# Attention scores spread by matmuls into PSUM instead of by two transfers through memory

## The chip, the core and the metric

The kernel runs on one core of a Trainium2 chip. The engines of a core each take their instructions in the order in which the program wrote them, and wait for one another by semaphores: PE multiplies matrices into PSUM, DVE (VectorE) and ACT (ScalarE) work on SBUF and PSUM, POOL (GpSimd) issues gathers and scatters here, SP issues the plain transfers. The metric is the device time of one execution in microseconds (us): the median of the runs.

## What is computed

Four graph layers run one after the other over 10,000 nodes of 512 floats and 2,500 edges (`src`, `dst`), each followed by a layer norm. The change lies in the last one, attention over the edges of a node, in fp32:

```python
q, k, v = jnp.split(x @ W, [Fqk, 2 * Fqk], axis=-1)      # 8 heads of 64
aw = jnp.einsum('ehf,ehf->eh', qs, ks)                   # a score per edge and head
m = jax.ops.segment_max(aw, src, num_segments=n)         # maximum over the edges of a source node
e = jnp.exp(aw - m[src])
denom = jax.ops.segment_sum(e, src, num_segments=n)
alpha = e / denom[src]
out = jax.ops.segment_sum(alpha[:, :, None] * vs, src, num_segments=n)
```

## The kernel before

The edges are cut into T = 20 tiles of 128, one edge per partition. Phases follow one another: `message_phase` (names with m_), `dense_phase` (d_, 80 tiles of nodes), `aggregate_phase`, `edge_rows_phase` (e_), `values_phase` (f_), `attended_rows_phase` (o_). Everything here happens in `values_phase`, a software pipeline written out by hand: STEPS = 24 steps, and in a step each engine works for tiles of different age. With `a = step`, `b = step - 1`, `c = step - 2`, `d = step - 3`, `e = step - 4`:

- Tile a: POOL has gathered the sums of the third layer (L1489, six buffers ahead); PE turns them (`turn_sums`, L1525) and multiplies (`first`, L1544 and L1545); ACT takes logarithms (`logarithms`); DVE finishes the softplus (L1746, L1748).
- Tile b: PE's `second` (L1555, L1558) makes the rows of the third layer, ACT copies them to `y` (L1668), DVE takes the moments (L1754 to L1761), ACT normalises (`x3_rows`).
- Tile c: PE turns the normalised rows (`turn_x3`, L1535) and makes queries into the bank `p_qv`, later keys into the bank `p_k` (L1565 for both and for the values).
- Tile d: DVE multiplies queries and keys and reduces them to 8 scores per edge (`scores`, L1768, L1770). `tile_maximum` then needs, in every partition (edge), the scores of all 128 edges of the tile: it adds `away`, which is very negative for edges of another source node, and takes the maximum (L1779, L1785, L1789). ACT takes the exponential (`weights`, L1694), DVE weighs the values (L1796), PE sums them over equal sources (`tile_sums`, L1594) into `p_S`, two banks.
- Tile e: DVE merges the tile's sums into the running state of a node (`new_maximum` L1804, L1809; `merge` L1817, L1821, L1827). POOL scatters the state to memory (L1500) and, once that has landed, gathers that of the next tile (L1495).

Between these, 40 "pairs" (256 rows of nodes without attention) pass through the same engines: load (L1123, L1124), four wide DVE operations and moments (L1138 to L1161), normalisation on ACT (L1103 to L1171) and store (L1130). `plain_plan` gives steps 0 and 1 three pairs, steps 2 and 3 two, and from step 4 on two and one in turn; DVE does one pair around `weigh_values` and the others at the end of its step, behind `softplus`. p_S holds two banks; p_qv, p_k, p_O, p_R and two p_T take the other six.

The path of the scores from one partition each to all partitions is SP's:

```python
sp.wait_ge(aw_done, t + 1)
sp.dma_start(k.aw_rows[t, :].rearrange("(h p) -> p h", h=HEADS), k.scores[:, t, :]).then_inc(aw_out, 16)
sp.wait_ge(aw_out, 16 * (t + 1))
...
sp.dma_start(spread[:, :, :]..., k.aw_rows[t:t + 1, :].to_broadcast([P, P * HEADS])).then_inc(spread_in, 16)
```

The first transfer writes 1,024 single floats to memory in transposed order; the second reads that row into all 128 partitions. SP's loads and stores of pairs stand behind the two in its queue.

Of the kernel before, what the change touches and what calls it, by code (L numbers as in the profile page):

```python
# [557 lines left out]
def dense_phase(nc, k):  # L558

    k.state = nc.dram_tensor("state", [ROWS, STATE], F32).ap()  # L560
    k.aw_rows = nc.dram_tensor("aw_rows", [EDGE_TILES, P * HEADS], F32).ap()
# [822 lines left out]
def values_phase(nc, k):  # L1384
# [3 lines left out]
    with phase(nc, "f_") as (sb, ps, sem), ExitStack() as ctx:  # L1388
# [11 lines left out]
        spread, prod, q = slots(0, 8).rearrange("p (h e) -> p h e", h=HEADS), slots(8, KB), slots(12, KB)  # L1400
# [4 lines left out]
        away = sb("away", [P, P])  # L1405
# [14 lines left out]
        q_done, q_out, k_done, prod_done, aw_done, aw_out, spread_in, away_done, cand_done, top_done, less_done = (  # L1420
            sem(n) for n in ("q_done", "q_out", "k_done", "prod", "aw", "aw_out", "spread_in", "away", "cand", "top",
                             "less"))
# [23 lines left out]
        def _(sp):  # L1446
# [7 lines left out]
            for step in range(STEPS):  # L1454
                here = HERE[step - 1] if step else 0
                if here > 2:
                    for j in range(pair, pair + here):
                        pair_load(nc, k, sp, j + 2)
                        pair_store(nc, k, sp, j)
                t = step - 3  # L1460
                if 0 <= t < T:
                    sp.wait_ge(aw_done, t + 1)
                    sp.dma_start(k.aw_rows[t, :].rearrange("(h p) -> p h", h=HEADS), k.scores[:, t, :]
                                 ).then_inc(aw_out, 16)
                    sp.wait_ge(aw_out, 16 * (t + 1))
                    if t:
                        sp.wait_ge(cand_done, t)
                    sp.dma_start(spread[:, :, :].rearrange("p h e -> p (h e)"),
                                 k.aw_rows[t:t + 1, :].to_broadcast([P, P * HEADS])).then_inc(spread_in, 16)
                if here <= 2:  # L1470
                    for j in range(pair, pair + here):
                        if j + 2 < PAIRS:
                            pair_load(nc, k, sp, j + 2)
                    for j in range(pair, pair + here):
                        pair_store(nc, k, sp, j)
                pair += here
# [7 lines left out]
        def _(pool):  # L1484
# [20 lines left out]
            gather_state(0)  # L1505
            for step in range(STEPS):
# [11 lines left out]
        def _(pe):  # L1518
# [56 lines left out]
            def keys(t):  # L1575
                pe.wait_ge(turned_out, turn_number(t + 2, 1) + 1)
                if t:
                    pe.wait_ge(prod_done, t)
# [495 lines left out]
```

## Time and profile before

| | us |
|---|---|
| runs, median of 3 | 2539.53 (2536.27 to 2550.1) |
| the profiled execution | 2559.03 |
| its span in the profile | 2557.3 |
| PE busy in the span | 1912.6 |
| DVE busy | 1569.5 |
| ACT busy | 1055.6 |
| POOL busy | 932.2 |

The span is that of one core; 1.7 us of the profiled execution lie outside it. A busy share is a mean over phases which have different limits, so it doesn't tell what bounds one phase. In the trace a tile's name is that of its buffer: `spread`, `prod`, `q` and `srcT` lie in the old buffer `same_dst`, `cand` in `filters`, `dstT` in `column_acc`. PE's rows come in pairs: one fp32 product is two matmul records. "idle before <- releaser" names what ended an engine's idle time.

### The profile page before, as it was taken

What the parts mean: (1) busy time and instruction counts of PE and PEld (TensorE: products, weight loads), DVE (VectorE), ACT (ScalarE), POOL (GpSimd) and SP (SyncE); (2) the same over time, 40 slices, a digit from 0 to 9 for tenths busy, and PEclk for the clock granted to TensorE, in tenths of its full rate; (3) what the DMA queues carried; (4) which work ended last, traced back from release to release, by engine and by line L of the source; (5) the groups of instructions that cost most, each with busy time, mean ns of one, the idle gap of its engine ahead of it and who ended that gap; (6) DMA issues with size and microseconds to landing.
All of it is one profiled execution on the core that took longest, in us unless ns stands there. A gap on an engine that the chain in (4) does not pass through costs nothing. (4 is left out here: it accounts for less than half of the span.)

```text
span 2557.3 us, 23979 instructions
## 1 busy us (share of the span) xinstructions
PE 1912.6 (75%) x5496; PEld 953.9 (37%) x5496; DVE 1569.5 (61%) x2664; ACT 1055.6 (41%) x2019; POOL 932.2 (36%) x1055
## 2 busy tenths in 40 slices
PE   5999995999999999999978603545766666677400
PEld 3444442444444444444434302332333333333200
DVE  5465451777777777777742437976555555555564
ACT  2344342555555555555543212434443333343122
POOL 2211012666665666666646244642011111100023
PEclk9999997999999999999998855556878788888755
DMA  7731024444444444444426342426444444433433
GB/s 250 260 105 38 13 33 117 153 155 145 155 160 149 146 161 157 146 152 161 152 103 199 46 106 69 87 56 245 94 134 114 110 116 116 116 116 108 114 131 111
DMA packets 170013, 326.07 MB, mean 128 GB/s; under 512 B 39889, under 2 KB 53106, under 8 KB 169686
## 3 DMA queue, kind: packets, MB, share of 16 engines
q1 hardware_dynamic: 138438, 244.22, 28.1%
q0 software_dynamic: 28160, 76.53, 13.9%
q10 hardware_dynamic: 3344, 4.51, 0.5%
q8 instruction: 28, 0.46, 0.1%
q14 instruction: 43, 0.35, 0.1%
HBM read 185.35 MB, written 139.84 MB: 127 GB/s over the span
## 5 line engine op out<-in xcount | busy, mean ns | idle before, releaser
L661 PE MATMUL d_p_h<-w3a,d_xT 128*128 128x512 f32 x640 | 290.6, 597 | 25.4 <-DMA d_xT<-in_xT 25.4
L661 PE MATMUL d_p_o<-d_w,d_uT 128*128 128x512 f32 x640 | 289.7, 595 | 3.0 <-ACT d_uT L736 3.0
L661 PE MATMUL d_p_p<-d_wr,d_x1T 128*128 128x512 f32 x640 | 290.6, 597 | 0.0
L818 DVE TENSOR_TENSOR d_zz<-d_yg,d_xbeta 128x512 f32<-128x512 f32 x80 | 138.6, 1732 | 98.8 <-POOL d_yg L869 98.8
L550 POOL TENSOR_SCALAR d_small<-d_mv 128x1 f32<-128x1 f32 x160 | 81.8, 511 | 304.9 <-DVE d_mv L787 155.0
L661 PEld LDWEIGHTS d_p_h<-w3a,d_xT 128*128 128x128 f32 x640 | 122.6, 192 | 180.7 <-issue 180.7
L661 PEld LDWEIGHTS d_p_o<-d_w,d_uT 128*128 128x128 f32 x640 | 121.9, 191 | 156.6 <-issue 152.1
L1489 POOL DMA_INDIRECT f_sums<-sum,index x40 | 40.1, 1003 | 365.5 <-PE f_p_T L1525 354.5
L1594 PE MATMUL f_p_S<-f_both,same_src 128*128 128x260 f32 x80 | 36.8, 607 | 170.4 <-DVE f_both L1796 170.4
L661 PEld LDWEIGHTS d_p_p<-d_wr,d_x1T 128*128 128x128 f32 x640 | 116.6, 192 | 117.1 <-issue 117.1
L729 ACT ACTIVATE d_yn<-d_y,d_small 128x512 f32<-128x512 f32 x80 | 65.1, 813 | 230.4 <-POOL d_small L555 230.4
L1779 DVE TENSOR_TENSOR filters<-same_dst,f_away 128x1024 f32<-128x1024 f32 x20 | 24.5, 1225 | 220.7 <-DMA same_dst<-aw_rows 220.7
L282 PE MATMUL m_p_H<-m_xT,m_w 128*128 128x512 f32 x320 | 148.1, 618 | 4.8 <-ACT m_xT L323 4.8
L757 ACT ACTIVATE d_x<-d_zz,d_small 128x512 f32<-128x512 f32 x80 | 65.1, 814 | 178.8 <-POOL d_small L555 178.8
L499 DVE TENSOR_SCALAR m_h<-m_p_H,m_bias 128x512 f32<-128x512 f32 x40 | 30.0, 750 | 154.4 <-issue 98.6
L552 POOL TENSOR_TENSOR d_small<-d_small,minus_half 128x1 f32<-128x1 f32 x160 | 113.0, 706 | 13.3
L869 POOL TENSOR_TENSOR d_yg<-d_yn,d_gamma_row 128x512 f32<-128x512 f32 x80 | 115.8, 1448 | 0.0
L811 DVE TENSOR_SCALAR d_low<-d_h 128x512 f32<-128x512 f32 x80 | 111.3, 1391 | 2.7
L863 POOL TENSOR_TENSOR d_xb<-d_x,d_b_row 128x512 f32<-128x512 f32 x80 | 101.5, 1269 | 12.2 <-DMA d_x<-in_x 12.2
L376 ACT ACTIVATE m_den<-m_low 128x512 f32<-128x512 f32 x40 | 25.2, 630 | 189.5 <-DVE m_low L504 189.5
L850 POOL TENSOR_TENSOR d_xbeta<-d_x,d_beta_row 128x512 f32<-128x512 f32 x80 | 101.5, 1269 | 0.0
L211 POOL DMA_INDIRECT sum<-m_tile_sum,unique x20 | 31.2, 1559 | 191.3 <-ACT m_tile_sum L339 175.3
(250 smaller groups left out, 4265.1 us busy)
## 6 DMA issues: line engine op xcount, KB each, us to landing
state<-d_empty SPq DMA_DIRECT2D x80, 264.0 KB, 2.1
sum<-m_tile_sum SPq DMA_DIRECT2D x10, 2048.0 KB, 7.7
d_xT<-in_xT SPq DMA_DIRECT2D x80, 256.0 KB, 2.7
d_z<-sum SPq DMA_DIRECT2D x80, 256.0 KB, 2.9
d_x<-in_x SPq DMA_DIRECT2D x80, 256.0 KB, 3.0
x<-d_x SPq DMA_DIRECT2D x80, 256.0 KB, 2.0
p<-d_p SPq DMA_DIRECT2D x80, 256.0 KB, 2.0
pair_p<-p SPq DMA_DIRECT2D x40, 512.0 KB, 7.0
```

Of the source, the lines that this page charges most:

```text
L282: pe.matmul(out, w1[:, s * KB + b, cols], xT[:, g % 2, s, b, :], start=(s == 0 and b == 0), stop=False)
L550: nc.gpsimd.tensor_scalar(tmp, var, factor, add, ALU.mult, ALU.add).then_inc(done, 1)
L552: nc.gpsimd.tensor_tensor(rstd, tmp, k.minus_half[:, 0:1], ALU.pow).then_inc(done, 1)
L661: last = nc.tensor.matmul(out[:, :], lhsT[:, c, :], w[:, c, :], start=(c == 0), stop=(c == KB - 1))
L729: nc.scalar.activation(yn[b][:, :], y[b][:, :], ACT.Identity, bias=small[b][:, 0, 2:3], scale=small[b][:, 0, 1:2]).then_inc(yn_done, 1)
L757: nc.scalar.activation(x1[b][:, :], zz[b][:, :], ACT.Identity, bias=small[b][:, 1, 2:3], scale=small[b][:, 1, 1:2]).then_inc(x1_done, 1)
L811: nc.vector.tensor_scalar(low[b][:, :], h[b][:, :], MISH_ONE, None, ALU.min).then_inc(low_done, 1)
L818: nc.vector.tensor_tensor(zz[b][:, :], yg[b][:, :], xbeta[b][:, :], ALU.add).then_inc(zz_done, 1)
L850: nc.gpsimd.tensor_tensor(xbeta[b][:, :], x[b][:, :], beta_row[:, :], ALU.add).then_inc(xbeta_done, 1)
L863: nc.gpsimd.tensor_tensor(xb[b][:, :], x[b][:, :], b4_row[:, :], ALU.add).then_inc(xb_done, 1)
L869: nc.gpsimd.tensor_tensor(yg[b][:, :], yn[b][:, :], gamma_row[:, :], ALU.mult).then_inc(yg_done, 1)
L1489: pool.indirect_dma_start(sums[u % AHEAD][:, :], None, k.sum2[:, :], at_rows(k.index[:, u % 2, u // 2:u // 2 + 1])).then_inc(sums_in[u % A ...
```

## The change

The table `aw_rows`, its two transfers per tile and the buffer `spread` go. In their place:

- POOL writes, once, at the start of the phase, a selector `head_rows` of 8 partitions: for head h, row h is ones and the others are zero.
- `turn_scores` on PE transposes the tile's scores (128 x 8) into the first 8 partitions of `p_k`; `scores_out` on ACT copies them to `scoresT` (8 x 128) in SBUF; `spread_scores` on PE multiplies, for each head, the selector by `scoresT`, so that all 128 partitions of p_S hold the head's 128 scores: 8 products of 128 columns, into the two banks that `tile_sums` uses later in the step.
- DVE's L1779 reads p_S instead of SBUF. `tile_sums` waits for that (`cand_done`), `spread_scores` waits until the last tile's sums are merged (`part_done`), and `keys` waits for `scores_out`.
- SP's queue keeps only the pairs, now always load, store, load, store.

The PE queue in a step, from `turn_sums(a, 0)` to `tile_sums(d)`; f_p_qv is the bank of queries (from `same_dst`) and values (from `wv`). Before:

```order
L1525 MATMUL f_p_T<-ident,f_sums 64x128 x4
L1565 MATMUL f_p_qv<-filters,same_dst 128x512 x4
L1544 MATMUL f_p_O<-f_sumT,f_w1s 128x128
L1545 MATMUL f_p_O<-f_sumT,f_w1v 128x384
L1525 MATMUL f_p_T<-ident,f_sums 64x128 x4
L1565 MATMUL f_p_qv<-wv,column_acc 128x512 x4
L1544 MATMUL f_p_O<-f_sumT,f_w1s 128x128
L1545 MATMUL f_p_O<-f_sumT,f_w1v 128x384
L1565 MATMUL f_p_k<-filters,column_acc 128x512 x4
L1594 MATMUL f_p_S<-f_both,same_src 128x260 x2
```

Of the change (the lines of `values_phase` stand 11 lower, further down 4 higher), where f_scoresT is the turned scores and `same_dst` in that row the selector:

```order
L1514 MATMUL f_p_T<-ident,f_sums 64x128 x4
L1572 MATMUL f_p_k<-ident,scores 8x128
L1554 MATMUL f_p_qv<-filters,same_dst 128x512 x4
L1582 MATMUL f_p_S<-f_scoresT,same_dst 128x128 x8
L1533 MATMUL f_p_O<-f_sumT,f_w1s 128x128
L1534 MATMUL f_p_O<-f_sumT,f_w1v 128x384
L1514 MATMUL f_p_T<-ident,f_sums 64x128 x4
L1554 MATMUL f_p_qv<-wv,column_acc 128x512 x4
L1533 MATMUL f_p_O<-f_sumT,f_w1s 128x128
L1534 MATMUL f_p_O<-f_sumT,f_w1v 128x384
L1554 MATMUL f_p_k<-filters,column_acc 128x512 x4
L1598 MATMUL f_p_S<-f_both,same_src 128x260 x2
```

One transposition stands in front of the queries, and the 8 spreading products between the queries and `first`; everything behind them keeps its order.

SP's queue for one step with two pairs, before (rows L1123 and L1124 load a pair, L1130 stores one):

```order
L1463 DMA aw_rows<-scores 128x8x1
L1468 DMA same_dst<-aw_rows 128x1024
L1123 DMA pair_p<-p 128x1024
L1124 DMA pair_x<-x 128x1024
L1123 DMA pair_p<-p 128x1024
L1124 DMA pair_x<-x 128x1024
L1130 DMA out_rows<-pair_rows 128x1024 x2
```

and of the change, where the same issues are L1122, L1123 and L1129:

```order
L1122 DMA pair_p<-p 128x1024
L1123 DMA pair_x<-x 128x1024
L1129 DMA out_rows<-pair_rows 128x1024
L1122 DMA pair_p<-p 128x1024
L1123 DMA pair_x<-x 128x1024
L1129 DMA out_rows<-pair_rows 128x1024
```

The second pair's load now stands behind the first pair's store, and nothing stands in front of the first load.

```diff
--- before.py
+++ after.py
@@ -558,7 +558,6 @@
 def dense_phase(nc, k):
 
     k.state = nc.dram_tensor("state", [ROWS, STATE], F32).ap()
-    k.aw_rows = nc.dram_tensor("aw_rows", [EDGE_TILES, P * HEADS], F32).ap()
 
 
 
@@ -1397,12 +1396,12 @@
         neg, rstd, shift = ([sb(f"{n}{i}", [P, 2]) for i in range(2)] for n in ("neg", "rstd", "shift"))
 
         slots = lambda first, n: k.same_dst[:, first:first + n, :].rearrange("p t e -> p (t e)")
-        spread, prod, q = slots(0, 8).rearrange("p (h e) -> p h e", h=HEADS), slots(8, KB), slots(12, KB)
+        head_rows, prod, q = slots(0, 8).rearrange("p (h e) -> p h e", h=HEADS), slots(8, KB), slots(12, KB)
         srcT = k.same_dst[:, 16:20, :]
         dstT = [k.column_acc[:, i, :].rearrange("p (c e) -> p c e", c=KB) for i in range(2)]
         cand = k.filters[:, :, :, :].rearrange("p t c f -> p (t c f)")[:, KB * 2 * D:KB * 2 * D + HEADS * P].rearrange(
             "p (h e) -> p h e", h=HEADS)
-        away = sb("away", [P, P])
+        away, scoresT = sb("away", [P, P]), sb("scoresT", [HEADS, P])
         less, both = sb("less", [P, HEADS]), sb("both", [P, HEADS, HD + 1])
         old = [sb(f"old{i}", [P, STATE + HEADS]) for i in range(2)]
         new, part = sb("new", [P, STATE]), sb("part", [P, HEADS, HD + 1])
@@ -1417,9 +1416,10 @@
         turned, turned_out, first_done, first_out, logs_done, pos_done, ssp_done, second_done, y_done = (
             sem(n) for n in ("turned", "turned_out", "first", "first_out", "logs", "pos", "ssp", "second", "y"))
         st, mv_done, ready, sc, x3_done = (sem(n) for n in ("st", "mv", "ready", "sc", "x3"))
-        q_done, q_out, k_done, prod_done, aw_done, aw_out, spread_in, away_done, cand_done, top_done, less_done = (
-            sem(n) for n in ("q_done", "q_out", "k_done", "prod", "aw", "aw_out", "spread_in", "away", "cand", "top",
-                             "less"))
+        q_done, q_out, k_done, prod_done, aw_done, aw_turned, aw_out, spread_done, away_done, cand_done = (
+            sem(n) for n in ("q_done", "q_out", "k_done", "prod", "aw", "aw_turned", "aw_out", "spread", "away",
+                             "cand"))
+        top_done, less_done, heads_set = (sem(n) for n in ("top", "less", "heads_set"))
         weighed, v_done, vw_done, s_done, old_in, new_top, fall_done, factors, scaled, part_done, merged, gone = (
             sem(n) for n in ("weighed", "v_done", "vw", "s_done", "old_in", "new_top", "fall", "factors", "scaled",
                              "part", "merged", "gone"))
@@ -1453,26 +1453,10 @@
             pair = 0
             for step in range(STEPS):
                 here = HERE[step - 1] if step else 0
-                if here > 2:
-                    for j in range(pair, pair + here):
+                for j in range(pair, pair + here):
+                    if j + 2 < PAIRS:
                         pair_load(nc, k, sp, j + 2)
-                        pair_store(nc, k, sp, j)
-                t = step - 3
-                if 0 <= t < T:
-                    sp.wait_ge(aw_done, t + 1)
-                    sp.dma_start(k.aw_rows[t, :].rearrange("(h p) -> p h", h=HEADS), k.scores[:, t, :]
-                                 ).then_inc(aw_out, 16)
-                    sp.wait_ge(aw_out, 16 * (t + 1))
-                    if t:
-                        sp.wait_ge(cand_done, t)
-                    sp.dma_start(spread[:, :, :].rearrange("p h e -> p (h e)"),
-                                 k.aw_rows[t:t + 1, :].to_broadcast([P, P * HEADS])).then_inc(spread_in, 16)
-                if here <= 2:
-                    for j in range(pair, pair + here):
-                        if j + 2 < PAIRS:
-                            pair_load(nc, k, sp, j + 2)
-                    for j in range(pair, pair + here):
-                        pair_store(nc, k, sp, j)
+                    pair_store(nc, k, sp, j)
                 pair += here
             while pair < PAIRS:
                 pair_store(nc, k, sp, pair)
@@ -1503,6 +1487,11 @@
             for u in range(AHEAD):
                 gather_sums(u)
             gather_state(0)
+            nc.gpsimd.memset(head_rows[0:HEADS, :, :], 0.0).then_inc(heads_set, 1)
+            pool.wait_ge(heads_set, 1)
+            nc.gpsimd.affine_select(head_rows[0:HEADS, :, :], head_rows[0:HEADS, :, :], pattern=[[1, HEADS], [0, P]],
+                                    base=0, channel_multiplier=-1, compare_op=ALU.not_equal, fill=1.0
+                                    ).then_inc(heads_set, 1)
             for step in range(STEPS):
                 for u in (2 * step + AHEAD, 2 * step + AHEAD + 1):
                     if u < 2 * T:
@@ -1575,8 +1564,24 @@
             def keys(t):
                 pe.wait_ge(turned_out, turn_number(t + 2, 1) + 1)
                 if t:
-                    pe.wait_ge(prod_done, t)
+                    pe.wait_ge(aw_out, t)
                 product(p_k, dstT[t % 2], k.wqk[:, :, D:2 * D], k_done)
+
+            def turn_scores(t):
+                pe.wait_ge(aw_done, t + 1)
+                nc.tensor.transpose(p_k[0:HEADS, 0:P], k.scores[:, t, :], k.ident[:, :]).then_inc(aw_turned, 1)
+
+            def spread_scores(t):
+
+                pe.wait_ge(aw_out, t + 1)
+                if t:
+                    pe.wait_ge(part_done, t)
+                else:
+                    pe.wait_ge(heads_set, 2)
+                for h in range(HEADS):
+                    last = nc.tensor.matmul(p_S[:, h // 4, (h % 4) * P:(h % 4 + 1) * P], head_rows[0:HEADS, h, :],
+                                            scoresT[:, :], start=True, stop=True)
+                last.then_inc(spread_done, 1)
 
             def values(t):
                 pe.wait_ge(q_out, min(t + 2, T))
@@ -1587,8 +1592,7 @@
             def tile_sums(t):
                 pe.wait_ge(vw_done, t + 1)
                 pe.wait_ge(weighed, t + 1)
-                if t:
-                    pe.wait_ge(part_done, t)
+                pe.wait_ge(cand_done, t + 1)
                 for half in range(2):
                     hs = slice(half * HEADS // 2, (half + 1) * HEADS // 2)
                     last = nc.tensor.matmul(p_S[:, half, 0:ATT // 2].rearrange("p (h f) -> p h f", h=HEADS // 2),
@@ -1607,10 +1611,14 @@
                     second(b, 1)
                 if a < T:
                     turn_sums(a, 0)
+                if 0 <= d < T:
+                    turn_scores(d)
                 if 0 <= c < T:
                     if c == 0:
                         pe.wait_ge(k.wqk_in, 32)
                     queries(c)
+                if 0 <= d < T:
+                    spread_scores(d)
                 if a < T:
                     first(a, 0)
                     turn_sums(a, 1)
@@ -1680,6 +1688,12 @@
                 if t:
                     act.wait_ge(prod_done, t)
                 nc.scalar.activation(q[:, :], p_qv[:, :], ACT.Copy, scale=float(HD) ** -0.5).then_inc(q_out, 1)
+
+            def scores_out(t):
+                act.wait_ge(aw_turned, t + 1)
+                if t:
+                    act.wait_ge(spread_done, t)
+                nc.scalar.activation(scoresT[:, :], p_k[0:HEADS, 0:P], ACT.Copy).then_inc(aw_out, 1)
 
             def away_from(t):
                 if t:
@@ -1717,6 +1731,8 @@
                     second_product_out(b, 1)
                 if a < T:
                     sums_turned_out(a, 0)
+                if 0 <= d < T:
+                    scores_out(d)
                 for _ in range(max(late - 1, min(late, 1))):
                     pair_normalise(nc, k, act, pair)
                     pair += 1
@@ -1772,11 +1788,11 @@
 
             def tile_maximum(t):
                 top = old[t % 2][:, STATE:STATE + HEADS]
-                dve.wait_ge(spread_in, 16 * (t + 1))
+                dve.wait_ge(spread_done, t + 1)
                 dve.wait_ge(away_done, t + 1)
                 if t:
                     dve.wait_ge(top_done, t)
-                nc.vector.tensor_tensor(cand[:, :, :], spread[:, :, :],
+                nc.vector.tensor_tensor(cand[:, :, :], p_S[:, :, :].rearrange("p a (h e) -> p (a h) e", h=HEADS // 2),
                                         away[:, :].rearrange("p (a e) -> p a e", a=1).to_broadcast([P, HEADS, P]),
                                         ALU.add).then_inc(cand_done, 1)
                 dve.wait_ge(cand_done, t + 1)
```

## Rows read from the trace of the kernel before

**Rows 1.** The line L1779: what ended DVE's idle time before it, us, times.

```profile
  DMA same_dst<-aw_rows: 220.7, 20
```

**Rows 2.** The line L1748 (`softplus`), from 1790 to 2360 us.

```profile
L1748 DVE SCALAR_TENSOR_TENSOR f_outT<-f_logs,f_pos x18: 424/426/426, 1796.3 to 2352.1; 128x256 f32<-128x256 f32 x18
```

**Rows 3.** Timeline of DVE, two steps; first columns: start us, us.

```profile
1920.48 1.23 DVE L1779 TENSOR_TENSOR filters<-same_dst,f_away 128x1024 f32<-128x1024 f32 x1 [8.56 <-DMA same_dst<-aw_rows]
...
1930.53 0.43 DVE L1748 SCALAR_TENSOR_TENSOR f_outT<-f_logs,f_pos 128x256 f32<-128x256 f32 x1
...
1938.87 0.16 DVE L1804 TENSOR_TENSOR f_new<-f_old 128x8 f32<-128x8 f32 x1
...
1940.58 0.69 DVE L1821 TENSOR_TENSOR f_part<-f_p_S,f_factor 128x520 f32<-128x520 f32 x1
...
1956.33 1.23 DVE L1779 TENSOR_TENSOR filters<-same_dst,f_away 128x1024 f32<-128x1024 f32 x1 [13.23 <-DMA same_dst<-aw_rows]
```

**Rows 4.** Timeline of SP's queue, 1938 to 1951 us.

```profile
1938.98 0.38 SPq L1463 DMA_DIRECT2D aw_rows<-scores  x1
1950.15 0.32 SPq L1468 DMA_DIRECT2D same_dst<-aw_rows  x1
```

**Rows 5.** Timeline of PE, one step and the start of the next.

```profile
1927.47 1.15 PE L1594 MATMUL f_p_S<-f_both,same_src 128*128 128x260 f32 x4 [3.71 <-DVE f_both L1796]
1931.01 2.08 PE L1555 MATMUL f_p_R<-src_rows_sb,ident 128*128 128x512 f32 x2 [2.39 <-DVE f_outT L1748]
...
1934.58 1.06 PE L1535 MATMUL f_p_T<-ident,src_rows_sb 128*128 128x128 f32 x4
...
1936.14 1.02 PE L1555 MATMUL f_p_R<-dst_rows_sb,ident 128*128 128x512 f32 x2
...
1937.22 0.83 PE L1558 MATMUL f_p_R<-f_w2v,f_outT 128*128 128x128 f32 x6
1937.89 0.60 PE L1525 MATMUL f_p_T<-ident,f_sums 128*64 128x128 f32 x4
1938.32 3.60 PE L1565 MATMUL f_p_qv<-filters,same_dst 128*128 128x512 f32 x8
1941.85 0.49 PE L1544 MATMUL f_p_O<-f_sumT,f_w1s 64*128 64x128 f32 x2
...
1948.16 3.70 PE L1565 MATMUL f_p_k<-filters,column_acc 128*128 128x512 f32 x8
```

**Rows 6.** Timeline of POOL, 1945 to 1954 us.

```profile
1945.07 0.99 POOL L1500 DMA_INDIRECT state<-f_new,unique  x1 [0.30 <-issue]
1953.18 0.97 POOL L1495 DMA_INDIRECT f_old<-state,index  x1 [7.12 <-DMA state<-f_new,unique]
```

**Rows 7.** DMA, 1820.84 to 2431 us; median us from issue to landing last.

```profile
DMA packets 39680, 70.91 MB, mean 116 GB/s; under 512 B 22511, under 2 KB 22511, under 8 KB 39654
...
f_old<-state,index POOLq DMA_INDIRECT x19, 7.0
```

**Rows 8.** Windows: us, then busy PE, PEld, DVE, ACT, POOL, then PEclk, DMA share.

```profile
1891.20:1920.48 29.28, 20.07 (x65) 11.76 (x66) 15.72 (x28) 14.01 (x33) 2.88 (x3) 0.71 0.48 144
1920.48:1956.33 35.85, 25.29 (x80) 13.23 (x78) 21.93 (x36) 11.33 (x27) 4.92 (x5) 0.90 0.46 91
```

**Rows 9.** Groups by form, 1820.84 to 2431 us: x count | busy us, mean ns.

```profile
L1821 DVE TENSOR_TENSOR f_part<-f_p_S,f_factor 128x520 f32<-128x520 f32 x19 | 13.2, 692 | 0.0
L1817 DVE TENSOR_TENSOR f_new<-f_old,f_factor 128x520 f32<-128x520 f32 x19 | 13.1, 691 | 5.6 <-ACT f_factor L1700 5.6
```

**Rows 10.** Timeline of DVE, 2360 to 2432 us: the last waits.

```profile
2369.55 1.22 DVE L1779 TENSOR_TENSOR filters<-same_dst,f_away 128x1024 f32<-128x1024 f32 x1 [8.29 <-DMA same_dst<-aw_rows]
...
2402.82 1.22 DVE L1779 TENSOR_TENSOR filters<-same_dst,f_away 128x1024 f32<-128x1024 f32 x1 [12.80 <-DMA same_dst<-aw_rows]
...
2431.02 1.23 DVE L1779 TENSOR_TENSOR filters<-same_dst,f_away 128x1024 f32<-128x1024 f32 x1 [13.38 <-DMA same_dst<-aw_rows]
```

## The prediction

> **What bounds the kernel now.** I read the page's table of busy times first, then the slices, the waits, and the timelines of DVE, SP, PE and POOL inside `values_phase`. No engine is busy throughout that phase. DVE sits idle in front of one line, L1779, for 220.7 us in 20 waits, and a transfer ends every one of them [rows 1]. In the timeline the wait is 8.56 us in one step and 13.23 us in the next [rows 3]. SP's rows tell why: the scores leave at 1938.98, the second transfer can be issued only at 1950.15, and its data let DVE start at 1956.33, so the way through memory takes 17.4 us [rows 3, 4]. DVE covers part of it with its own work up to 1943.1 (1956.33 less the wait).
>
> The phase has a loop. `softplus` (L1748) ends at S = 1930.96 [rows 3]; PE starts `second` at 1931.01, 0.05 later [rows 5]; everything behind it on PE follows, and DVE's L1779 is followed without a gap by 10.5 us of work up to the next `softplus` end (1920.48 to 1930.96) [rows 3]. I therefore count in intervals from one `softplus` end to the next. There are 17, from 1796.3 to 2352.1, 555.8 us in all or 32.7 each [rows 2]: ten "long" ones, which begin with DVE's extra pair, and seven "short" ones. Three more waits come after them [rows 10].
>
> **What the change does, part by part.** Times below are us after S.
>
> *Long interval.* The scores are ready at 8.0 (SP's issue at 1938.98) [rows 4]. PE, at full clock, gets to `turn_scores` earlier: `second` takes 1.75 (1936.14 to 1937.89), the turned rows 1.56, `second` again 1.75, `turn_sums` 0.43, in all 5.5 [rows 5]. So the new wait stands in PE's queue with the queries behind it, and costs PE 2.5. Nothing in the trace shows the transposition of 8 columns; four of 64 columns take 0.43 together, so it lies between 0.1 and 0.43, and I take 0.25. The copy on ACT (8 x 128) runs beside the queries, which take 3.53, and is covered by them. Queries: 8.25 to 11.8. The 8 spreading products have 128 columns and a weight load each, as the three of `second` that take 0.67 from start to start, 0.22 each; with the 0.16 that the last needs to drain, 8 take 2.0. At half clock it would be twice that, so the bounds are 2.0 and 4.0; I take 2.0, since no idle time stands in front of them. Spread ends at 13.8. DVE is ready at 12.1 (1943.1), so a wait of 1.7 stays of 13.2, and `softplus` ends at 13.8 + 10.5 = 24.3. PE needs from the end of the queries to the end of the keys 10.0 (1941.85 to 1951.86), then 1.15 for `tile_sums` [rows 5]: 13.8 + 10.0 + 1.15 = 25.0. **PE ends last, so a long interval takes 25.0.**
>
> *Short interval.* No pair is ahead of the scores, PE doesn't wait: 5.5 + 0.25 + 3.53 = 9.3. Now the state's loop comes in. POOL's scatter was issued 3.2 after the queries' end (1945.07), its gather at 1953.18, and the gather lands 7.0 after that [rows 6, 7]: 18.3 after the end of whatever stands in front of `first`. In the long interval before, that is 13.8 + 18.3 = 32.1, or 7.1 in this one. From L1804 to the end of L1821 (`part_done`, for which the spreading waits) are 2.4 (1938.87 to 1941.27) [rows 3], giving 9.5. Spread 9.5 to 11.5, `softplus` at 22.0, PE at 11.5 + 11.15 = 22.7. **A short interval takes 22.7.** Before a long one the same sum gives 11.5 + 18.3 - 22.7 = 7.1, under the 7.9 at which DVE gets to L1804: no wait.
>
> *Sum over the intervals.* 10 x 25.0 + 7 x 22.7 = 408.9, against 555.8: 146.9 less. I give back 0.5 per interval, 8.5, for stretches at half clock and handoffs that I counted at 0.05: 138.4.
>
> *The last three waits* are 8.29, 12.80 and 13.38 [rows 10]. First: spread ends at 11.5 where L1779 started 17.0 after S: 5.5 less. Second: PE has idled, so I put the queries at 5.3 (between 3.5 and 7.1) and the way at 8.5 with copy and spread, of which DVE's merge covers 2.7: 5.8 stay, 7.0 less. Third: no queries, half clock: 4.4, of which 1.7 stay, 11.7 less. Together 24.2.
>
> *What costs nothing.* POOL's selector (two instructions on 8 partitions) is made at the phase's start, three steps before its first use, with POOL idle behind its first gathers; were it late, only the first of 20 waits would feel it. ACT's copy costs the pairs' normalisation behind it some 0.3 per step, with slack of several us before `query_out` is needed for the values. L1779 now reads PSUM: the same product from PSUM takes 692 ns and from SBUF 691 [rows 9], so nothing. The Trainium skill, "VectorE: DVE Perf Modes", section on the TRN2 errata, has 120 fixed cycles for a PSUM source against 58 for SBUF at 0.96 GHz, which speaks against this change: by it the sum would be worse by 20 x 0.065 = 1.3 us; the rows don't show it. The first pair's store and the second's load change places in SP's queue; the load is needed a whole interval later.
>
> **Total: 138.4 + 24.2 = 162.6 us less.** The profiled execution of 2559.0 would become 2396.4. That one lies 19.5 above the median of 2539.5, so on the median the forecast is **2377 us** (-6.4%). Of the 220.7 idle us, some 60 come back as PE's time: after the change PE and DVE bound the phase together, and neither the transfers nor ACT.
>
> **Rivals.**
>
> *The state's loop becomes the bound.* Scatter and gather already arrive 7.1 after S in a short interval. If they land 4 later (more traffic per us), short intervals grow by 4 and long ones by 1.5: 43 us, so 2420. For it: both are on the path with almost no slack. Against: 22,511 of 39,680 packets are under 512 bytes [rows 7], nearly all of them the 1,024 single floats of the transfer that goes. Chance 0.12.
>
> *PE starts intervals at half clock.* The window with PE busy 20.07 of 29.28 us had a granted clock of 0.71, that with 25.29 of 35.85 had 0.90 [rows 8]; `second` after a gap took 3.57 (1931.01 to 1934.58) for what takes 1.75 [rows 5]. If that stays, 1.8 per interval over 17: 31 us, 2408. The Trainium skill, "TensorE: Matmul & The Clock Gate", section "HAM oscillation", says that matmul work which repeatedly waits for a transfer goes back to half rate each time; by that rule the gaps' disappearance would end it, my 8.5 would not be given back, and the result would be 2368. The rows agree in direction. Chance of the rival 0.12.
>
> *Better than replayed.* If the gather lands sooner and the products overlap (spread 1.5), and the allowance isn't needed, 20 more are saved: 2357. Chance 0.10.
>
> *The pairs' transfers were hidden by the waits.* The phase moves 70.91 MB at a mean of 116 GB/s, less 10 MB now [rows 7]. Were 116 its limit, the 610 us would shrink only to 528 (61.2 MB), that is by 82: 2457. Against: in single windows it moved 144 GB/s [rows 8]. Chance 0.04.
>
> *No change.* The transfers' wait is replaced by another of the same length on DVE, for instance `old_in` at 12: 2540. Nothing points to it. Chance 0.03.
>
> *Slower: PE at half clock throughout, with its new work.* From `turn_scores` to the end of `tile_sums` PE needs 16.9 at full clock; at 1.2 GHz twice that, and with the 8.0 in front 41.9 per interval against 32.7: 17 x 9.2 = 156 more, 2696. It decides once 8.0 + 16.9 / clock passes 32.7, at a granted clock under 0.68. The trace has 0.71 with more idle time than there will be. Chance 0.02.
>
> **How the numbers follow.** The forecast has 0.57. The time is its own, 2377. The range goes from 2345 (a bit under the better replay) to 2435, which takes in the first two rivals and leaves out the last three and the tails, some 0.15. Its lower end also takes the lower bounds of transposition and spread, its upper end the upper ones (2.2 x 17 = 37 us). Half a per cent is about what a measurement of this kernel can tell from no change. Faster 0.95, same 0.03, slower 0.02.
>
> **What would show it.** Right: L1779's wait falls from 11 us to 1 to 3 and PE ends it; intervals alternate at about 25 and 23; the granted clock of the phase rises above 0.85; the phases before and after keep their times. In a long interval PE waits some 2.5 before the transposition, in a short one DVE waits for `old_in` before L1804. Wrong: L1804 released by the gather at 10 or later (the state's loop), a granted clock at 0.8 or lower in the intervals (the second rival), DVE waiting for loads of pairs (the fourth).

## The result, and the profile after

| | before | changed |
|---|---|---|
| median of 4 runs, us | 2537.9 (2536.0 to 2550.1) | 2391.48 (2384.89 to 2393.1) |
| ratio | | 0.9409, 95% interval 0.9373 to 0.9444 |
| the profiled execution | 2559.03 | 2384.89 |
| its span | 2557.3 | 2383.1 |

The forecast was 2377 with a range of 2345 to 2435; the changed kernel takes 2391. The page's first lines of the changed kernel:

```profile
span 2383.1 us, 24662 instructions
...
PE 1924.1 (81%) x5836; PEld 969.6 (41%) x5836; DVE 1570.6 (66%) x2664; ACT 1060.0 (44%) x2039; POOL 942.3 (40%) x1057
```

Busy times hardly moved, PE's by 11.5 us. What went is idle time. The same line of DVE as in [rows 1], now L1795, with its own durations:

```profile
L1795 DVE TENSOR_TENSOR filters<-f_p_S,f_away x20: 1224/1225/1226, 1808.7 to 2257.8; 128x1024 f32<-128x1024 f32 x20
...
  PE f_p_S L1582: 66.1, 20
```

The wait fell from 220.7 to 66.1 us, and PE ends all 20. The sum itself takes 1225 ns from PSUM as it took from SBUF [rows 3]. The intervals, counted as in [rows 2] from the line of `softplus`:

```profile
L1764 DVE SCALAR_TENSOR_TENSOR f_outT<-f_logs,f_pos x18: 424/426/426, 1794.5 to 2203.1; 128x256 f32<-128x256 f32 x18
```

From 1794.5 to 2203.1 the 17 intervals take 408.6 us, against 555.8: 147.2 less. From the last of them to the last L1795 (2257.76, below) the tail takes 54.7, against 78.9 (2431.02 less 2352.1): 24.2 less. The starts differ by 1.8 and the end of the program by 1.0. Together that is the 174.2 us by which the two spans differ.

One long and one short interval of the changed kernel on DVE (start us, us), to set beside [rows 3]:

```profile
1906.41 1.22 DVE L1795 TENSOR_TENSOR filters<-f_p_S,f_away 128x1024 f32<-128x1024 f32 x1 [3.40 <-PE f_p_S L1582]
...
1916.46 0.43 DVE L1764 SCALAR_TENSOR_TENSOR f_outT<-f_logs,f_pos 128x256 f32<-128x256 f32 x1
...
1918.13 0.16 DVE L1820 TENSOR_TENSOR f_new<-f_old 128x8 f32<-128x8 f32 x1
...
1927.72 1.22 DVE L1795 TENSOR_TENSOR filters<-f_p_S,f_away 128x1024 f32<-128x1024 f32 x1 [3.88 <-PE f_p_S L1582]
...
1937.77 0.43 DVE L1764 SCALAR_TENSOR_TENSOR f_outT<-f_logs,f_pos 128x256 f32<-128x256 f32 x1
```

and on PE, beside [rows 5] (L1572 transposes, L1554 with f_p_qv<-filters is the queries, L1582 spreads, L1598 is `tile_sums`, L1544 opens `second`):

```profile
1895.54 0.60 PE L1514 MATMUL f_p_T<-ident,f_sums 128*64 128x128 f32 x4
1898.93 0.27 PE L1572 MATMUL f_p_k<-ident,scores 128*8 128x128 f32 x1 [2.79 <-DVE scores L1786]
1899.04 5.36 PE L1554 MATMUL f_p_qv<-filters,same_dst 128*128 128x512 f32 x8
1904.33 2.05 PE L1582 MATMUL f_p_S<-f_scoresT,same_dst 8*128 8x128 f32 x16
1906.30 0.49 PE L1533 MATMUL f_p_O<-f_sumT,f_w1s 64*128 64x128 f32 x2
...
1915.96 1.04 PE L1598 MATMUL f_p_S<-f_both,same_src 128*128 128x260 f32 x4
1916.94 1.12 PE L1544 MATMUL f_p_R<-src_rows_sb,ident 128*128 128x512 f32 x2
...
1922.00 0.27 PE L1572 MATMUL f_p_k<-ident,scores 128*8 128x128 f32 x1
1922.11 3.60 PE L1554 MATMUL f_p_qv<-filters,same_dst 128*128 128x512 f32 x8
1925.64 2.05 PE L1582 MATMUL f_p_S<-f_scoresT,same_dst 8*128 8x128 f32 x16
...
1937.27 1.04 PE L1598 MATMUL f_p_S<-f_both,same_src 128*128 128x260 f32 x4
1938.25 1.13 PE L1544 MATMUL f_p_R<-src_rows_sb,ident 128*128 128x512 f32 x2
```

In the long interval PE waits 2.79 us for the scores, its queries then take 5.36 instead of 3.60, and the spreading ends at 1906.3. In the short one nothing stops PE. At both ends `second` starts 0.05 us behind the end of `softplus` (1916.89 and 1938.20), and also right behind `tile_sums`: PE and DVE arrive together. This long interval, from 1890.87, takes 26.0 and the short one 21.3, in all 47.3. Others split differently, as here (start us, us, PE again):

```profile
1995.55 0.27 PE L1572 MATMUL f_p_k<-ident,scores 128*8 128x128 f32 x1 [1.84 <-DVE scores L1786]
1995.66 3.66 PE L1554 MATMUL f_p_qv<-filters,same_dst 128*128 128x512 f32 x8
1999.26 2.05 PE L1582 MATMUL f_p_S<-f_scoresT,same_dst 8*128 8x128 f32 x16
...
2012.53 1.04 PE L1598 MATMUL f_p_S<-f_both,same_src 128*128 128x260 f32 x4
2013.40 1.02 PE L1544 MATMUL f_p_R<-src_rows_sb,ident 128*128 128x512 f32 x2
...
2025.50 5.30 PE L1554 MATMUL f_p_qv<-wv,column_acc 128*128 128x512 f32 x8
```

Here PE waited 1.84 in the long interval, its queries took 3.66, and the slow products are the values, 4.49 in this interval (at 2003.51) and 5.30 in the short one behind it. The intervals there are 24.8 and 22.8, in all 47.6. Here PE ends last: `softplus` was over at 2012.27, and `second` starts at 2013.40, 0.87 behind the start of `tile_sums`. At the ends of the first pair it started 0.98 behind it, so there DVE was the last, by 0.1 us. Of the 17 intervals nine end like the first pair and eight like this one.

The state's loop on POOL, beside [rows 6], and the transfers of the phase, beside [rows 7] (last number: median us to landing):

```profile
1909.52 1.57 POOL L1484 DMA_INDIRECT state<-f_new,unique  x1 [0.30 <-issue]
1913.15 0.97 POOL L1479 DMA_INDIRECT f_old<-state,index  x1 [2.05 <-DMA state<-f_new,unique]
```

```profile
DMA packets 16907, 59.88 MB, mean 136 GB/s; under 512 B 2416, under 2 KB 2416, under 8 KB 16880
...
state<-f_new,unique POOLq DMA_INDIRECT x19, 3.4
f_old<-state,index POOLq DMA_INDIRECT x19, 3.5
```

The scatter lands in 3.4 us where it needed some 7 to 8, the gather in 3.5 instead of 7.0, and nine in ten of the packets under 512 bytes are gone. The phase's window before and now (length, then PE busy; the granted clock, third from the end, goes from 0.80 to 0.93), and the last three waits, beside [rows 10]:

```profile
1820.84:2431.00 610.16, 403.26 (x1256) 218.19 (x1256) 356.96 (x589) 228.50 (x549) 64.27 (x64) 0.80 0.42 116
...
1820.00:2260.00 440.00, 404.28 (x1569) 228.70 (x1569) 348.43 (x576) 225.90 (x550) 72.00 (x64) 0.93 0.40 136
```

```profile
2214.90 1.23 DVE L1795 TENSOR_TENSOR filters<-f_p_S,f_away 128x1024 f32<-128x1024 f32 x1 [3.24 <-PE f_p_S L1582]
...
2240.79 1.23 DVE L1795 TENSOR_TENSOR filters<-f_p_S,f_away 128x1024 f32<-128x1024 f32 x1 [5.41 <-PE f_p_S L1582]
...
2257.76 1.23 DVE L1795 TENSOR_TENSOR filters<-f_p_S,f_away 128x1024 f32<-128x1024 f32 x1 [3.12 <-PE f_p_S L1582]
```

### The profile page after: what moved, and what is told of

Same layout as the page of the kernel before. It is cut to its first block and busy times, and to the rows that moved or that the text cites. A ratio compares the mean times of both kernels' runs of the same rounds, so it can differ in the third digit from the quotient of the medians.

```text
span 2383.1 us, 24662 instructions
## 1 busy us (share of the span) xinstructions
PE 1924.1 (81%) x5836; PEld 969.6 (41%) x5836; DVE 1570.6 (66%) x2664; ACT 1060.0 (44%) x2039; POOL 942.3 (40%) x1057
## 5 line engine op out<-in xcount | busy, mean ns | idle before, releaser
L779 DVE TENSOR_TENSOR d_y<-d_p_o,d_xb 128x512 f32<-128x512 f32 x80 | 55.3, 692 | 66.4 <-PE d_p_o L660 66.4
L200 POOL DMA_INDIRECT m_x_in<-in_x,index x40 | 44.5, 1113 | 134.4 <-PE m_p_T L238 120.8
```

Source lines behind the costliest of these rows:

```text
L779: nc.vector.tensor_tensor(y[b][:, :], p_o[b][:, :], xb[b][:, :], ALU.add).then_inc(y_done, 1)
```

## Experiments

The experiments form three groups, each on a chip of its own, with the kernel before measured beside them: e1 to e4 (before took 2568.1 us), e5 to e8 (2560.7) and e9 to e11 (2566.9). So times are best compared within a group, and ratios to before across groups. Times are medians; in brackets stands the 95% interval of the ratio.

**e5: the changed kernel again, as a base.** No edit.

> The changed kernel itself, on the chip of the runs beside it, as their base: 2385 to 2400 us by every theory, since the runs with the old queue order gave 2394.

Measured: 2387.72 us, ratio to before 0.9333 (0.9316 to 0.9350).

**e1: the old traffic, which no computing engine waits for.** Both transfers are issued again, with SP's queue in its old order; the broadcast goes into 96 unused partitions and reads a row of x. SP waits only for the last tile's broadcast before it issues the next. An excerpt:

```diff
+                t = step - 3
+                if 0 <= t < T:
+                    sp.wait_ge(aw_done, t + 1)
+                    sp.dma_start(k.aw_rows[t, :].rearrange("(h p) -> p h", h=HEADS), k.scores[:, t, :]
+                                 ).then_inc(junk_out, 16)
...
+                    sp.dma_start(junk, k.x[2 * t:2 * t + 2, :]...to_broadcast([96, P * HEADS])).then_inc(junk_in, 16)
```

> The changed kernel, with both old transfers issued again for every tile (the 1,024 single floats to memory, and a broadcast of 4 KB, here into 96 partitions of unused space), but nothing waits for them; SP's queue in its old order. Theory 1 (the gain is the way through memory taken out of DVE's path; its traffic is beside the point): scatter and gather of the state land later again, and only short intervals feel it, by 1 us or less: 2391 to 2403 us. Theory 2 (a good part of the gain is relief of the DMA engines, whose packets under 512 bytes went from 22,511 to 2,416): 2420 us or more, with DVE waiting for the state or for pairs.

Measured: 2482.61 us, 0.9661 (0.9628 to 0.9694). Theory 1 falls in its strict form: 88 us over e4, which has the same queue order without the traffic. If the traffic had stayed, half of the gain of 174 us would be gone. This is no share that could be added to others: with the way gone and the traffic there, e1 gains 85 us over before; with the single floats gone and a way through memory kept, e2 gains 137; without floats and without the way it is 174 (e4).

**e4: only SP's old queue order.** In a step with two pairs again load, load, store, store.

```diff
+                    for j in range(pair, pair + here):
                         if j + 2 < PAIRS:
                             pair_load(nc, k, sp, j + 2)
-                        pair_store(nc, k, sp, j)
+                    for j in range(pair, pair + here):
+                        pair_store(nc, k, sp, j)
```

> The changed kernel with SP's queue in the old order (in a step with two pairs: load, load, store, store). Theory 1: no difference within 5 us. Rival (the new order of loads and stores is worth something by itself): 10 us or more slower, with DVE waiting for stores at the pairs' sum.

Measured: 2394.40 us, 0.9322 (0.9284 to 0.9360). The order is worth nothing that shows: its interval overlaps that of e5.

**e6: the single floats alone.** e1 without the broadcast and its waits.

```diff
-                    sp.dma_start(junk, k.x[2 * t:2 * t + 2, :]...to_broadcast([96, P * HEADS])).then_inc(junk_in, 16)
```

> The changed kernel, with only the first of the old transfers issued again for every tile (the 1,024 single floats to memory, nobody waits for them), queue order as of old. With both transfers it took 2482.6 us, 88 more than with none. Theory 2a: the single floats hold up the rings on which the pairs' loads stand behind them, and nearly all of the 88 us are theirs: 2460 us or more, DVE still waits for pairs' loads. Theory 2b: the 88 us come from the bytes of the broadcast: 2410 us or less here.

Measured: 2474.77 us, 0.9674 (0.9657 to 0.9691). 4 KB per tile, cut into 1,024 packets, cost 87 us over e5; adding 384 KB of broadcast costs nothing that shows, by the overlapping intervals of e1 and e6. Transfers of e6, with the median to landing last, then the same rows of e5, then DVE's wait in e6 (us in total, times, longest):

```profile
DMA packets 29848, 50.32 MB, mean 114 GB/s; under 512 B 17689, under 2 KB 17689, under 8 KB 29823
...
pair_p<-p SPq DMA_DIRECT2D x23, 512.0 KB, 14.0
...
state<-f_new,unique POOLq DMA_INDIRECT x15, 7.7
```

```profile
pair_p<-p SPq DMA_DIRECT2D x29, 512.0 KB, 4.5
...
state<-f_new,unique POOLq DMA_INDIRECT x19, 3.4
```

```profile
DVE pair_p L1138 <- DMA pair_p<-p: 47.1, 9, 6.6
```

A pair's load lands after 14.0 us instead of 4.5, and DVE waits 47.1 us for it, which it did nowhere in e5; the kernel before waited for a load once, 1.0 us. The scatter is back at 7.7, but that isn't tied to the floats alone: it takes 6.8 in e2, which has none of them, and 4.1 in e10, which has them all.

**e9: the same 4 KB as 8 rows.** As e6, but from the transposed scores, so that SP waits for ACT's copy instead of for the scores. ACT also waits, before it overwrites `scoresT`, until the last tile's rows have landed. An excerpt:

```diff
-                    sp.wait_ge(aw_done, t + 1)
-                    sp.dma_start(k.aw_rows[t, :].rearrange("(h p) -> p h", h=HEADS), k.scores[:, t, :]
+                    sp.wait_ge(aw_out, t + 1)
+                    sp.dma_start(k.aw_rows[t, :].rearrange("(h p) -> h p", h=HEADS), scoresT[:, :]
```

> As the run with the single floats alone (2474.8 us), with the same place in SP's queue and a wait for the tile's scores there, but the 4 KB leave as 8 rows of 512 bytes from the transposed scores. Theory 2a (the 1,024 packets of 4 bytes hold up the rings, on which the pairs' loads stand behind them): back to 2387 to 2400 us, and a pair's load lands some 5 us after its issue instead of 14. Rival (what cost the 87 us is SP's wait for the scores in front of the loads): 2450 us or more, loads landing soon but issued late.

Measured: 2386.39 us, 0.9294 (0.9280 to 0.9308): all 87 us are gone, with as many bytes, the same place in the queue and a wait for the tile's scores in front of the loads. The cost lay in how the bytes are cut; whether the number of the packets or their size of 4 bytes counts isn't told apart. Its transfers:

```profile
DMA packets 16683, 58.12 MB, mean 132 GB/s; under 512 B 2496, under 2 KB 2640, under 8 KB 16656
...
state<-f_new,unique POOLq DMA_INDIRECT x18, 3.4
```

**e10: the single floats behind the pairs.** As e6, but issued at the end of SP's step.

> The single floats again, nobody waits for them, but issued at the end of SP's step, behind the loads and stores of its pairs and so 10 to 15 us before the next loads are needed. Theory 2a with slack (a late load costs only where DVE wants it at once): the loads still take about 14 us to land, but DVE hardly waits; 2395 to 2420 us. Rival (the floats cost by their occupation of the DMA engines wherever they stand, through the state's scatter and gather too): 2450 us or more.

Measured: 2413.28 us, 0.9425 (0.9377 to 0.9473), some 25 over e5 instead of 87. So most of the cost hangs on the place of the floats in SP's queue. The reason isn't shown in full: the next step's load is still often issued right behind the floats (at 1932.27 behind 1931.79), and when it lands isn't on record. What the trace has is that DVE waits for no load any more. It now waits here (us in total, times, longest):

```profile
DVE pair_rows L1152 <- DMA out_rows<-pair_rows: 25.3, 10, 10.9
DVE f_new L1834 <- DMA f_old<-state,index: 19.1, 7, 3.6
```

that is for stores of pairs and for the state's gather. One wait for a store alone took 10.9 us.

**e2: through memory, but in rows.** PE transposes and ACT copies as in the changed kernel; then SP, its queue in the old order, writes `scoresT` as 8 rows and broadcasts them into SBUF. PE's spreading products are left out, which changes nothing in what is computed. An excerpt:

```diff
+                    sp.wait_ge(aw_out, t + 1)
+                    sp.dma_start(k.aw_rows[t, :].rearrange("(h p) -> h p", h=HEADS), scoresT[:, :]
+                                 ).then_inc(written, 16)
+                    sp.wait_ge(written, 16 * (t + 1))
...
-                if 0 <= d < T:
-                    spread_scores(d)
```

> PE still transposes the scores and ACT copies them, but then they go through memory: 8 rows of 512 bytes are written, and broadcast back into SBUF; PE's 8 spreading products are left out. Theory 1: the way through memory falls from 17.4 us to about 9 (write 2.5, issue, broadcast 4.5, and the handoffs), since the 11 us of the write came from its single floats; a pair of intervals takes about 52 us against 47.3 with the change and 65 before, so about 2440 us. Rival (the length of the write comes from the receipt by memory, whatever its packets): the write still takes some 10 us, and the kernel some 2500 us or more.

Measured: 2431.18 us, 0.9449 (0.9419 to 0.9478). SP's queue and DVE's line, to set beside [rows 4] and [rows 3]:

```profile
1972.43 0.29 SPq L1465 DMA_DIRECT2D aw_rows<-f_scoresT  x1
1973.67 0.32 SPq L1470 DMA_DIRECT2D same_dst<-aw_rows  x1
```

```profile
1977.93 1.23 DVE L1807 TENSOR_TENSOR filters<-same_dst,f_away 128x1024 f32<-128x1024 f32 x1 [3.02 <-DMA same_dst<-aw_rows]
```

The second transfer can be issued 1.24 us after the first, where it took 11.17. From the issue of the write to DVE's line are 5.5 us instead of 17.4; the transposition and ACT's copy now stand in front of that. A transposition and a write in rows alone would have brought 137 us of the 174 by which e4 beats before on the same chip; staying in PSUM brings the other 37.

**e3: the spreading twice.** The second set of products writes the same values again.

```diff
-                for h in range(HEADS):
+                for h in list(range(HEADS)) * 2:
```

> The changed kernel with the 8 spreading products issued twice over. Theory 1 (PE's queue is the bound after the change): each of 20 steps grows by the 2.0 us of the products, 2391 + 40 = 2431 us. Rival (DVE or the state's loop is the bound, PE has slack in it): under 15 us more.

Measured: 2436.21 us, 0.9486 (0.9440 to 0.9532): 42 over e4, where 20 times 2.0 are 40. So the spreading stands on the path with its full length, and the rival with slack is out. It doesn't tell PE from DVE behind it: L1795 waits for the second set too, so DVE's share of the interval starts later by as much as PE's. In this trace `second` starts 1.1 us behind `softplus` at the end of all 17 intervals, so PE ends last in each; in the changed kernel it did in eight.

**e7: queries ahead of the scores in long intervals.** In the steps behind two pairs PE no longer stands idle in front of the transposition, and `first(a, 0)` comes ahead of the spreading:

```diff
-                if 0 <= d < T:
+                behind = step and HERE[step - 1] > 1
+                if 0 <= d < T and not behind:
                     turn_scores(d)
...
                     queries(c)
+                if 0 <= d < T and behind:
+                    turn_scores(d)
+                if a < T and behind:
+                    first(a, 0)
                 if 0 <= d < T:
                     spread_scores(d)
                 if a < T:
-                    first(a, 0)
+                    if not behind:
+                        first(a, 0)
```

> The changed kernel, but in the steps behind two pairs PE does the queries first, then turns the scores, does the first product of `first`, and then spreads. Theory 1 (PE's queue is the bound, and its wait of 1.8 to 2.8 us for the scores in long intervals is lost time): long intervals fall from 25 or 26 us to about 23, so about 22 us less, 2366 to 2376 us. Rival (DVE takes over at once, since the maximum comes later): under 5 us less.

Measured: 2366.93 us, 0.9244 (0.9223 to 0.9264), 21 less than e5 and clear of its interval. It beats both kernels. In e5 PE waited ten times for the scores, 22.4 us in all, and the granted clock of 1820 to 2220 is 0.95 here and 0.94 there: what is gained is the wait rather than the clock. In the trace, a long interval's products (queries, transposition, spreading), and the one wait for scores that is left:

```profile
2080.23 3.60 PE L1554 MATMUL f_p_qv<-filters,same_dst 128*128 128x512 f32 x8
2083.67 0.27 PE L1572 MATMUL f_p_k<-ident,scores 128*8 128x128 f32 x1
...
2084.93 2.05 PE L1582 MATMUL f_p_S<-f_scoresT,same_dst 8*128 8x128 f32 x16
```

```profile
PE f_p_k L1572 <- DVE scores L1792: 4.9, 1, 4.9
```

**e8: unused products in the gap.** Eleven of them ahead of the wait for the scores, in each of the eleven steps behind two pairs:

```diff
+                if 0 <= d < T and 0 <= c < T and HERE[step - 1] > 1:
+                    pe.wait_ge(vw_done, c - 1)
+                    pe.wait_ge(q_out, c)
+                    for _ in range(11):
+                        nc.tensor.matmul(p_qv[:, 0:P], k.ident[:, :], k.ident[:, :], start=True, stop=True)
```

> The changed kernel, with 11 unused products of 128 columns (2.5 us at 2.4 GHz) ahead of the wait for the scores in long intervals, so that PE isn't idle there. If PE's idle gap is what makes the clock fall (queries of 5.36 us instead of 3.53 behind a gap of 2.79), the products cost nothing and save up to 1.8 us in each of ten long intervals: 2372 to 2385 us, granted clock up. If the half-rate stretches come whether or not PE was idle (one came in an interval without a gap), no gain or a loss of some us, and the same clock.

Measured: 2376.73 us, 0.9289 (0.9270 to 0.9308), 11 less than e5. PE in e8 (the fillers, the transposition, the queries), then windows of 400 us of e8 and of e5 (granted clock third from the end):

```profile
1895.97 2.62 PE L1618 MATMUL f_p_qv<-ident 128*128 128x128 f32 x22
1898.92 0.27 PE L1572 MATMUL f_p_k<-ident,scores 128*8 128x128 f32 x1 [0.33 <-DVE scores L1791]
1899.03 3.66 PE L1554 MATMUL f_p_qv<-filters,same_dst 128*128 128x512 f32 x8
```

```profile
1820.00:2220.00 400.00, 391.74 (x1726) 235.83 (x1724) 329.33 (x549) 217.09 (x526) 68.59 (x60) 0.98 0.40 139
```

```profile
1820.00:2220.00 400.00, 378.98 (x1489) 215.10 (x1489) 318.58 (x531) 214.51 (x523) 66.37 (x60) 0.94 0.40 136
```

Behind the fillers the queries take 3.66, and in no interval more, and the clock of the stretch is 0.98 instead of 0.94. The gap cost the clock; that useless work makes the kernel faster shows it by itself. Slow values remain, as 5.20 at 1927.53.

**e11: e7 and four fillers ahead of steps with one pair.** Added to e7:

```diff
+                if 4 < step < T and HERE[step - 1] == 1:
+                    for _ in range(4):
+                        nc.tensor.matmul(p_qv[:, 0:P], k.ident[:, :], k.ident[:, :], start=True, stop=True)
```

> Queries first in long intervals (2366.9 us), and 4 unused products ahead of the steps in which PE waits some 1.0 us for softplus. If gaps of 1 us still drop the clock, the half-rate stretches go and some 5 to 10 us with them: 2355 to 2362 us. If those stretches come without a gap, no gain or 5 us more, since PE is the bound: 2366 to 2372 us.

Measured: 2369.06 us, 0.9236 (0.9221 to 0.9250), the same as e7. It is a weak test of gaps of 1 us: e7's trace has only three waits of 1.0 us for `softplus` in the intervals, so most of the fillers stand where there was no gap, and one such wait (at 1821.05) comes before the first of them. The slow values stay, as 5.29 at 1904.16 and 2043.74.

## Why the prediction was right

**The sum.** The forecast had 146.9 for the intervals before its allowance, and 147.2 came; it had 24.2 for the last three waits, and 24.2 came, though the waits themselves shrank by 5.1, 7.4 and 10.3 where 5.5, 7.0 and 11.7 stood. So in the profiled executions the change brought 174 where 162.6 stood, and the difference is the allowance of 8.5 and the shift of the start and the end. That the intervals were met so closely is luck, as the terms show.

**Its terms, one by one.** The transposition was put at 0.25: the queries start 0.11 behind it. The 8 products were put at 2.0: 1.97 (1904.33 to 1906.30). PE's wait in a long interval was put at 2.5: it was 2.8 six times, 1.8 three times and 0.2 once. The ten long intervals take 254.0 together, 25.4 each, against 25.0; the seven short ones 154.6, or 22.1 each, against 22.7. So 4.0 too little and 4.3 too much cancelled. Reading PSUM costs L1795 nothing: 1225 ns on either side. The Trainium skill, "VectorE: DVE Perf Modes", section on the TRN2 errata, has more fixed cycles for a PSUM source than for SBUF; the 1.3 us that I had estimated from that page didn't appear.

Two terms of PE were put too long. The 5.5 us in front of the transposition came from a stretch in which the turned rows took 1.56 (1934.58 to 1936.14), with four transposes at 1.06 where they now take 0.60; from the start of `second` to the transposition it is 5.06 now (1916.94 to 1922.00). And from the end of the spreading to the next `second` I had 10.0 + 1.15 = 11.15: with the values at full rate it takes 10.64 (1906.30 to 1916.94). So "PE ends last" holds for only eight of the 17 intervals, those with slow values in them; in nine DVE's 10.5 behind L1795 ended last, by 0.1. A long interval without a slow product takes 24.3 (1845.24 to 1869.55) and a short one 21.3; at these lengths all 17 would take 392. The other 16 us up to 408.6 are the half clock, below, for which the allowance had 8.5 along with the handoffs.

Two of my signs failed too. L1795 was to wait 1 to 3 us: the mean is 3.3 (66.1 / 20). And DVE was to wait for `old_in` before L1820 in short intervals: no such wait is in the trace.

**The step that was wrong: the transfers that stay keep their durations.** The working took the scatter's and gather's 8.1 and 7.0 us from the old trace [rows 6, 7] and put the gather's landing at 7.1 of a short interval, as something that sets `part_done`. They now take 3.6 and 3.5, DVE reaches L1820 at 1918.13 without a wait, and the loop isn't near the bound. The prediction saw the single floats leave, and used that only against a rival. e6, e9 and e10 show what they would cost in the changed kernel: 87 us, if they stand ahead of the pairs' loads. It nearly cancelled: the short interval would have come out at 22.45 by PE alone (9.3 + 2.0 + 11.15), the difference being 0.25. That the sum held doesn't mean that the account of the gain held. In the old kernel they had no wait of their own: DVE waited for a pair's load only once there, 1.0 us, and the floats stood inside the 220.7 us that it waited anyway [rows 1], as the 11.17 us between SP's two issues [rows 4].

**The half clock.** The second rival was put at 1.8 per interval throughout. The trace has slow stretches of that size in part of the intervals (5.36 and 5.30 against 3.60), and a granted clock of 0.93 in the phase; e8 wins 11 us by filling eleven gaps. The long interval's 26.0 is this rival. I had the queries at full clock, 3.53, directly behind a wait that my own sum put at 2.5, and gave the half clock only to the products behind them as a bound. Behind the six waits of 2.8 us the queries took 5.36 five times.

The section "HAM oscillation" of the Trainium skill's "TensorE: Matmul & The Clock Gate" says that work which repeatedly waits for a transfer falls back to half rate. The trace agrees in direction: with shorter waits the phase's clock is 0.93, where it was 0.80. My rival by it, 2368 with no half rate left, didn't come: one part of the slow stretches stands behind the wait that the change opens on PE, another part has no gap in front of it.

**The carry-over to the median.** The profile's difference was 174.2, the medians' 146.4. The forecast subtracted 19.5, the amount by which the old profiled execution lay above its median; the new one lies 6.6 below its own. Those 26.1 us are more than the 14.5 by which 2377 was too low; the profiled execution, 11.5 under its forecast of 2396.4, took the rest back. In the experiments the kernel before took 2561 to 2568 and the changed one 2388, on one chip a difference of 173. Why the old kernel's time moves by up to 30 us from one group of runs to another and the new one's by 4 is open; nothing tried here tells it.

**The other rivals.** The pairs' transfers weren't limited by bytes: the phase moves 136 GB/s now. No other wait took the old one's place at its length, and PE at half clock throughout didn't come: 0.93.

## What to carry to other kernels

A tiny transfer can be the most expensive one: count its packets, not its bytes, and look at what stands behind it in the same queue; transposing on PE first and writing rows took the write from 11 us to 1. If a round trip through memory leaves a path, re-time the transfers that stay before summing. And where an engine that is about to become the bound gets a new wait in the middle of its queue, put work that doesn't need the result in front of it: that brought another 21 us here.

## What the runs showed that I had not expected

- 1,024 packets of 4 bytes, 4 KB in all, made a 512 KB load behind them land after 14.0 us instead of 4.5 (e6). The scatter on another queue took 7.7 there instead of 3.4, though e2 and e10 show that this depends on more than the floats. As 8 rows of 512 bytes the same data cost nothing that shows.
- PE's rate fell also where no gap stood in front: at 2025.50 the values took 5.30 instead of 3.60, and the last idle time on PE before that was the 1.84 us that ended at 1995.55. Such stretches stayed in e7, e8 and e11. What triggers them is open.
